# Cross-attention and a mixture of experts on one core: a batch's four row scatters issued at three places of a round instead of one

## What is computed

```
x = x + attention(layernorm(x), ctx)            # per batch, softmax over 77 keys
logits = layernorm(x) @ router_w                # 8 experts
top_w, top_i = top_k(softmax(logits), 2)
for e in range(8):
    h = silu(xn @ gate_w[e]) * (xn @ up_w[e])   # F = 1024
    out = out + cw[:, e:e+1] * (h @ down_w[e])
x = x + out
```

## Time and profile before

| | us |
|---|---|
| median of 3 runs | 1013.5 |
| lowest, highest | 1013.02, 1018.3 |
| the profiled execution, its own time | 1013.09 |
| its span in the trace | 1011.3 |
| first and last of the 64 row scatters start at | 97.9, 425.0 |
| a full round between 136 and 327 us (start to start of L969) | 23.8 to 24.0 |

### The profile page before, as it was taken

The page is one execution under the profiler, slowest core; times in us unless marked ns, Lnnn a source line. Parts: engine busy times, 40 slices in busy tenths (PEclk is TensorE's granted clock), DMA queues, the critical chain, the costliest instruction groups (busy, mean ns, idle before and its releaser), DMA issues.

```text
span 1011.3 us, 32130 instructions
## 1 busy us (share of the span) xinstructions
PE 895.4 (89%) x12208; PEld 795.6 (79%) x12208; DVE 628.1 (62%) x1930; ACT 472.4 (47%) x891; POOL 290.0 (29%) x337
## 2 busy tenths in 40 slices
PE   3899888888888886199999999999999999999996
PEld 2667666666666664088999999999999999999995
DVE  7789767777777775355745644744754756644443
ACT  2677666666666674143523423532432434423221
POOL 4566733333333322502211211211212212211111
PEclk9998888888888886589999999999999999999998
DMA  4312222121211331216252522242252252222221
GB/s 144 109 42 67 61 70 65 59 59 59 59 59 59 111 120 53 93 44 179 38 151 54 152 36 54 51 137 53 33 156 53 33 156 55 33 35 36 36 32 16
DMA packets 69072, 73.57 MB, mean 73 GB/s; under 512 B 19724, under 2 KB 62810, under 8 KB 69018
## 3 DMA queue, kind: packets, MB, share of 16 engines
q1 hardware_dynamic: 44666, 32.94, 11.4%
q0 software_dynamic: 12944, 17.87, 10.2%
q10 hardware_dynamic: 11408, 22.06, 6.2%
HBM read 45.18 MB, written 26.39 MB: 71 GB/s over the span
## 4 chain that ended last, share of the span: by engine, by line
PE 50%; DMA 4%; issue 4%; DVE 3%; ACT 3%; POOL 1%; ACTq 0%; another core or an unknown queue 0%; SPq 0%; POOLq 0%; DVEq 0%
PE bank L483 11%; PE bank L485 11%; PE bank L484 11%; PE bank L681 5%; PE bank L683 5%; PE bank L682 5%; DMA raw<-expert_rows 4%; PE bank L656 1%; PE bank L544 1%; POOL expert_rows L1385 1%; DVE h_full L1252 1%; ACT h_hi L830 1%; ACT g_act L828 1%; DVE e_lo L1117 1%; ACT pt_hi L758 1%
## 5 line engine op out<-in xcount | busy, mean ns | idle before, releaser
L483 PE MATMUL bank<-xg,e_hi 128*128 128x128 f16 x2176 | 373.3, 220 | 0.7 <-DVE xg L1229 0.6
L484 PE MATMUL bank<-xg,e_hi 128*128 128x128 f16 x2176 | 373.3, 220 | 0.0
L485 PE MATMUL bank<-xg,e_lo 128*128 128x128 f16 x2176 | 373.3, 220 | 0.0
L1416 POOL DMA_INDIRECT out<-y_sb,tok_row x68 | 113.4, 1668 | 466.6 <-DVE y_sb L1247 443.1
L483 PEld LDWEIGHTS bank<-xg,e_hi 128*128 128x128 f16 x2176 | 213.5, 98 | 2.0 <-issue 0.8
L484 PEld LDWEIGHTS bank<-xg,e_hi 128*128 128x128 f16 x2176 | 213.5, 98 | 0.7
L485 PEld LDWEIGHTS bank<-xg,e_lo 128*128 128x128 f16 x2176 | 213.5, 98 | 0.0
L828 ACT ACTIVATE g_act<-bank 128x512 f32<-128x512 f32 x136 | 81.3, 598 | 249.3 <-PE bank L485 233.9
L1252 DVE SCALAR_TENSOR_TENSOR h_full<-bank,g_act 128x512 f32<-128x512 f32 x136 | 94.0, 691 | 128.7 <-ACT g_act L828 121.0
L681 PE MATMUL bank<-e_hi,h_hi 128*128 128x256 f16 x544 | 148.4, 273 | 4.1 <-DVE h_lo L1258 4.1
L683 PE MATMUL bank<-e_hi,h_lo 128*128 128x256 f16 x544 | 148.3, 273 | 0.0
(11 more groups left out here) (175 smaller groups left out, 1850.6 us busy)
## 6 DMA issues: line engine op xcount, KB each, us to landing
raw<-expert_rows SPq DMA_DIRECT2D x68, 132.5 KB, 2.5
e_stage<-in_gate_w ACTq DMA_DIRECT2D x7, 1024.0 KB
e_stage<-in_up_w ACTq DMA_DIRECT2D x7, 1024.0 KB
e_stage<-in_down_w ACTq DMA_DIRECT2D x7, 1024.0 KB
expert_rows<-pads SPq DMA_DIRECT2D x8, 530.0 KB
xin<-in_x SPq DMA_DIRECT2D x16, 256.0 KB, 2.8
xres<-in_x SPq DMA_DIRECT2D x16, 256.0 KB
out<-x SPq DMA_DIRECT2D x16, 256.0 KB
```

Of the source, the lines that this page charges most:

```text
L483: pe.matmul(dst, a_hi(c), b_hi(c), start=c == 0, stop=False)
L484: pe.matmul(dst, a_hi(c), b_lo(c), start=False, stop=False)
L485: mm = pe.matmul(dst, a_lo(c), b_hi(c), start=False, stop=ends and c == chunks - 1)
L1416: pool.indirect_dma_start(out, bass.IndirectOffsetOnAxis(tok_row[:], 0), y_sb[:], None, compute_op=ALU.add).then_inc(added, 16)
```

## The change

The four scatters of a batch are issued at three places of GpSimd's round, in rounds that have both `z` and `n` (5 to 15): one right behind `split_kv`, one behind `make_rows`, and two behind `split_cx`. Ahead of the last two a new function `landed` waits until the first two of this batch have landed. Rounds 16 to 20 issue all four together, as before. As a batch's scatters now come on both sides of the next batch's waits, `scattered` becomes two semaphores, one for even and one for odd batches. On DVE `take_slots` is started at unit 1, together with `combine_weights`, instead of unit 2, so the two chains take turns.

```diff
+def same_parity(j):
+    return At(j.plus // 2, j.reg, j.times // 2)
...
-        scattered = sem("scattered")
+        scattered = [sem("scattered_even"), sem("scattered_odd")]
...
-            sp.wait_ge(scattered, SCATTER * B)
+            for par in range(2):
+                sp.wait_ge(scattered[par], SCATTER * B // 2)
...
-                after(dve, scattered, r.value(SCATTER, -SCATTER))
+                after(dve, scattered[par], same_parity(r).value(SCATTER))
...
-                starts = {1: [(z, lambda j: start(weights_chain))],
-                          2: [(z, lambda j: start(slots_chain))],
+                starts = {1: [(z, lambda j: start(weights_chain)), (z, lambda j: start(slots_chain))],
...
-            def scatter(r, par):
-
-                after(pool, row_ready, r.value(2, 2))
-                after(pool, cw_ready, r.value(1, 1))
-                after(pool, slots_ready, r.value(1, 1))
+            def scatter(r, par, first, end):
+
+                if first == 0:
+                    after(pool, row_ready, r.value(2, 2))
+                    after(pool, cw_ready, r.value(1, 1))
+                    after(pool, slots_ready, r.value(1, 1))
                 apart(pool, passed)
-                for t in range(NT):
-                    for k in range(2):
-                        pool.indirect_dma_start(rows_dram, bass.IndirectOffsetOnAxis(slot_u[:, par, t, k:k + 1], 0),
-                                                rows[:, par, t, :], None).then_inc(scattered, 16)
+                for s in range(first, end):
+                    t, k = divmod(s, 2)
+                    pool.indirect_dma_start(rows_dram, bass.IndirectOffsetOnAxis(slot_u[:, par, t, k:k + 1], 0),
+                                            rows[:, par, t, :], None).then_inc(scattered[par], 16)
+
+            def landed(r, par, count):
+
+                pool.wait_ge(scattered[par], same_parity(r).value(SCATTER, 16 * count))
+                apart(pool, passed)
 
             def body(n, a, b, c, r, z):
                 if a:
                     split_kv(a, a.plus % 2)
+                if z and n:
+                    scatter(z, z.plus % 2, 0, 1)
                 if r:
                     make_rows(r, r.plus % 2)
+                if z and n:
+                    scatter(z, z.plus % 2, 1, 2)
                 if n:
                     split_cx(n)
...
-                if z:
-                    scatter(z, z.plus % 2)
+                if z and n:
+                    landed(z, z.plus % 2, 2)
+                    scatter(z, z.plus % 2, 2, 4)
+                if z and not n:
+                    scatter(z, z.plus % 2, 0, 2 * NT)
```

More of the change, by code:

```diff
@@ L1365, in make_rows @@
             def make_rows(j, par):
-                after(pool, scattered, j.value(SCATTER, -SCATTER))
+                after(pool, scattered[par], same_parity(j).value(SCATTER))
                 parts = rows[:, par, :, 0:D].bitcast(F16)
```

## The result

| us | before | changed |
|---|---|---|
| median, lowest to highest, 4 runs each | 1013.8, 1013.02 to 1018.3 | 980.5, 978.49 to 985.42 |
| the profiled execution, its span | 1013.09, 1011.3 | 978.49, 976.7 |
| mean granted clock of PE | 0.928 | 0.959 |

The account below looks back on a forecast made before the run. No engine is full; late PE posts during GpSimd's back-to-back scatters leave shared holes. Per round -2.63 + 0.2 + 0.2 + 1.2 = -1.0 us, -11 us over 11 rounds: 1013.1 to 1002 us, range 988 to 1015.

Parts of the forecast that it names:

- Rival B: Follow-up rival: the clock is the whole gain; both kernels' rounds at an unbroken clock are equally long; no chance given.
- The cause: Rounds 5 to 15: while GpSimd makes descriptors of scatters back to back, PE's posts are held back; `pt_hi` idles 2.63 us.
- The four together go: minus 2.63: Attention rounds 5 to 15: removing the row of four scatters takes away ACT's 2.63 us wait at `pt_hi` per round.
- The first and second scatter, 0.2 each: At their new, earlier places each makes posts none to 0.58 us late; taken as 0.2 us a round each.
- The rows, the split, the landing wait at nothing: GpSimd's low rows stay put, the context split slips 1.3 us, the landing wait delays nobody; each costs nothing.
- The pair, 1.2: Last two scatters hold posts 2.8 us from their start, leaving a hole between nothing and 2.63; taken as 1.2 us.
- DVE's order at 0: `slot` needs PE's ranks right behind `prob_sum`; costs between 0 and 0.2 us a round, taken as 0.
- The clock... So I count no gain: PE's clock falls once a round behind the hole, but round 4 without it has 0.84 against 0.86; no gain.
- hole goes whole, 991 us: Rival, chance 0.20: the pair holds no due post or PE works through; rounds match round 4, 2.0 us less each.
- the clock takes the gain: Second way of the nothing-changes rival (0.22 together): the clock's fall moves to full units, eating the 1.0 us; 1013 us.

Follow-up runs that it names:

- held and filled: Kernel before, ACT's sixth `pt_hi` held for a GpSimd memset behind the fourth scatter, 20 idle PE matmuls in the hole: 1002.9 us, 0.988.
- two pairs behind the split: Kernel before, all scatters behind the context's split, landing wait between first and last two, DVE's old order: 983.4 us, 0.969 late; 963.5 us, 1.005 quiet.
- spaced in place: Kernel before with a 0.7 us GpSimd memset behind each of the first three of a round's four scatters, nothing moved: 971.2 us, 0.957.

## Why the prediction was wrong

The direction, the cause and the places were right for a late chip; the size was a third of what came, and the step that failed is the clock, which I had counted at nothing. A full round, put together from the runs:

| | hole before `pt_hi` | clock | round, us |
|---|---|---|---|
| before, late chips | 2.6 | 0.86 | 23.8 to 24.0 |
| held and filled, late | 2.8 | 1.00 | 22.2 to 22.3 |
| changed, without landing wait, late | 1.0 | 0.85, 0.92 | 21.8 to 22.5 |
| changed, first chip, rounds 7 to 12 | 0.65, 1.25 | 1.00 | 20.1, 20.6 |
| two pairs behind the split, late | 1.0 to 1.6 | 1.00 | 20.3 to 20.9 |
| spaced in place, late | none | 1.00 | 19.5, 19.6 |
| order of before or of the change, quiet | none | 1.00 | 19.2, 19.4 |

From the first line to the second is the clock's part, 1.7 us on one chip; from there to the spaced one the hole's, 2.6 us, but that step goes from one late chip to another. The two pairs and the spaced kernel stand on one chip, both at a full clock: a hole of 1.0 to 1.6 us costs 0.8 to 1.4 us of a round. Rival B falls by that: at a full clock the hole still costs most of its length. Step by step:

- **The cause** (scatters in a row hold PE's posts): right on late chips. The spacing in the old place moves nothing and takes nothing away, and the hole is gone in all eleven rounds. The late waits of the change sum to half of before (9.7 for 20.3), as I had said. The rule that I set against it, of the Trainium skill's page "SBUF — State Buffer", section "Who interferes with whom" (PE and ACT never wait on anyone, DMA never contends with an engine), stands in a section on the ports of SBUF and says nothing of posts. On the quiet chips no wait is seen; on the late ones 0.957 speaks against using it for posts. Not every post is late there: in nine of the eleven full rounds of before, ACT's `probs` starts 0.03 to 0.04 us behind DVE's while the four scatters are being made.
- **"The four together go: minus 2.63"**: right, as far as two chips can be compared. With the clock full the round is 22.2 us with the hole on one and 19.5 to 19.6 without on another, 2.6 us apart.
- **The first and second scatter, 0.2 each**: too much. They started at 5.3 and 9.5 us of the round (I had 5.7 to 6.7, and 10.0), and little is lost behind them. The `pt_hi` 1.4 us behind the second starts 0.35 to 0.39 us behind its turn in rounds 8 to 13, where a quiet chip has 0.20 to 0.26, and waits for it in one round only (0.34 us, round 7).
- **The rows, the split, the landing wait at nothing**: right; nobody is late behind them. But the landing wait seems to have a worth, which I didn't look for: 0.967 with it on the first chip, 0.979 without on another.
- **The pair, 1.2**: measured 0.65 and 1.25 in turns, so 0.95 on average, and released 2.85 us behind its start, where I had estimated 2.8. Near enough.
- **DVE's order at 0**: right on both kinds of chip with the scatters at their old place (1.000 and 0.999). In the changed kernel on a quiet chip, undoing it gave 1.003 against 1.000.
- **"The clock... So I count no gain"**: this is the step that failed. By the terms above a round should have lost 2.63 - 0.95 = 1.7 us; it lost 3.5, and the other 1.8 is the clock, which the filled hole puts at 1.7. I had read round 4's 21.9 us and 0.84 as a round without the hole and with the clock's fall. But round 4 lasts 21.9 us at a clock of 1.00 as well. In that round DVE is the busiest engine at a full clock (19.1 and 19.9 us), and ACT and PE wait for its subtraction (4.5 to 6.1 and 2.4 us), so it has another limit and tells nothing of the other rounds.
- **The rival "hole goes whole, 991 us"** was priced from the same round 4, at 2.0 us a round. Its true price is 23.9 - 19.55 = 4.35, 48 us for eleven rounds; the spacing in place, in which two early rounds of 23.7 and 20.7 us are left, won 43.6. So the low end of my range, 988, was too high for the case that I had given a chance of 0.20.
- **The rival "the clock takes the gain"** had the sign wrong: the fall follows the hole and goes with it. In rounds 13 and 14, where it did come back, 1.8 and 1.4 us are still won.
- **What I could not have told**: that the effect is one of the chip. Nothing in one trace says so.

Open: what makes a chip late. Durations of scatters (0.96 to 1.14 us) and of their landing (2.5 to 3.3 us for the last ones) are the same on both kinds. And by what way a scatter delays a post of PE was not tried: the spacing moves the descriptor work and the transfers behind it alike, so the runs don't tell these two apart.

## What to carry to other kernels

Look for idle time whose producer ended long before, and see what GpSimd does at that moment. If it issues indirect DMAs back to back, try spacing them by other GpSimd work before reordering anything, and measure on more than one chip. Price a hole in a stage where PE is nearly full with the clock's fall that follows it, and take the price from a round of the same work; a round with a different mix of work is no baseline, however near its clock is.

## What the runs showed of the hardware

- On three of five chips, and in the first measurement, PE's posts come late while GpSimd issues scatters: 5.8 us behind the first of four, 2.8 us behind the first of two, 1.3 behind a single one, so about 1.4 us for each, by an estimate from these three. Posts of DVE to ACT come within 0.04 us in nine of eleven of the same bursts. On two chips PE's don't come late at all. The kernel before is 5.9% slower on one chip than on another (1014.8 against 958.5), and spacing the scatters alone wins back 43.6 of these 56 us.
- Behind a single scatter only a stretch is held: posts due 0.73 to 1.11 us behind its start came at 1.30 to 1.36, those due by 0.59 or from 1.37 on came within 0.05 us.
- At starts 1.27 to 1.48 us apart the delays add up; at 1.83 to 1.98 us apart `pt_hi` waited for no late post in a full round. The bound lies between; where, was not tried.
- A hole of 2.8 us in each round brings one fall of the clock to 1.2 GHz (0.50 granted) with it, unless PE has other matmuls in it (1.00). The fall costs 1.7 us of a round of 23.9. The length of the hole doesn't settle it: with holes of 1.0 us in each round the clock fell each time (0.85, 0.92), with 0.57 to 1.36 us in turns it stayed full for six rounds.
